# Two-layer graph network: the second feed-forward's residual and bias accumulated by TensorE beside its second product

## The chip, the cores and the metric

One core of a Trainium2 chip runs the whole program in one launch. The metric is the device time in microseconds, from start to end of the launch; lower is better. TensorE multiplies matrices (its weight loads are listed apart, as PEld), VectorE (DVE), ScalarE (ACT) and GpSimd (POOL) do the elementwise work, and SyncE (SP) issues most DMAs. Results of TensorE land in PSUM, eight banks of 512 f32 per partition.

## What is computed

3125 nodes with 128 features and 53125 edges go through two attention layers over the graph, each followed by a feed-forward block and a layer norm. The change sits in the second layer's last part:

```
h   = _ln(conv + x, g1, b1)                       # first norm
ffn = gelu(h @ Wf1 + bf1) @ Wf2 + bf2             # 128 -> 512 -> 128
y   = _ln(ffn + h, g2, b2)                        # second norm
out = _layernorm(x + y)                           # output norm
```

_ln subtracts the mean over the 128 features, divides by the root of the variance plus 1e-5, multiplies by g and adds b. x is the second layer's input. Everything is f32.

## The kernel before

Nodes are padded to 25 tiles of 128 (NB = 25), one node tile per block of 128 columns in X, Y and AGG; the text calls such a tile a node. "Quads" are groups of four nodes (the seventh has one). Every engine has its own instruction list, written out by hand; the order between engines is set by semaphores. `after(engine, name, n)` makes an engine wait until the semaphore has reached n, and an engine runs its list in order, so whatever stands behind a wait waits too.

For each of the two layers the program projects, gathers edges (26 rounds, the bulk of the time), sums them per node into AGG, and then runs the feed-forward over the nodes as a software pipeline: each engine has a loop over s, and handles node s plus or minus an offset in it. In the second layer the pieces are these.

- TensorE (loop `for s in range(-2, NB + 7)`): `widen(s+1)` (L956) makes the 512 hidden values of a node, four matmuls of 128x128 into one of two banks; `turn2(s+2)` (L951) transposes a normalised node into PS[1]; `attention` (L884) transposes the sums of a quad into PS[0], at every fourth s; `narrow(s)` (L964) is the second product, four matmuls accumulated into PS[6] (`ffn_of`). narrow waits for the gelus of its node and for `ffn_added` of the node before, since there is one tile for all.
- ScalarE: `turned2(s+1)` (L731) copies the transposed node with gain and bias of the first norm into hT2, `gelus(s)` (L739) makes four gelus, `normal2(s+5)` (L751) normalises a node in Y, with a shift that VectorE made, and `normalise_last(s-11)` (L758) makes the output rows.
- GpSimd: `inverse_root(i, b, w)` (L488) turns the variances of a quad into inverse roots, for norm 0, 1 and 2 (a, b and c in the semaphores' names); `affine(s+1)` (L538) multiplies Y by g1 and adds FB (b1 plus bf2, summed once at the end of layer one), which makes the residual in place, after turn2 has read the node.
- VectorE: `residual` (L1373), at every fourth s, adds the transposed sums of four nodes to the layer's input, takes their statistics (`node_stats`, L1384) and moments (`moments`, L1387); `add_ffn(s-1)` (L1412) adds the product in PSUM to Y and takes statistics; `scale_last(s-5)` (L1449) subtracts the mean and multiplies by g2; `add_input(s-6)` (L1454) multiplies by the inverse root, adds x and takes the statistics of the output norm; `shift_of` (L1397) makes minus mean times root for ScalarE.

`add_first_nodes` on VectorE belongs to the end of the edge rounds: it finishes the sums of the last round and already does the residual of the first two quads. SyncE stores output rows as ScalarE finishes them. The loop of the first layer shares turn2, widen, narrow and add_ffn by l == 0.

`skip_part` (L984) and `attention` of the first layer add a bias through TensorE: `ones3`, three rows, by the bias split into three bf16 parts, broadcast to 512 columns, ahead of f32 matmuls into the same bank.

Of the kernel before, what the change touches and what calls it, by code (L numbers as in the profile page):

```python
# [16 lines left out]
P = 128  # L17
# [26 lines left out]
def build(nc, a, out):  # L44
# [11 lines left out]
    with ExitStack() as ctx:  # L56
# [3 lines left out]
        def sem(name):  # L60
# [121 lines left out]
        attention_of, turned2_of, ffn_of, turned_of = PS[0], PS[1][:, 0:P], PS[6][:, 0:P], PS[7][:, 0:P]  # L182
# [13 lines left out]
            pc_ready act_col count_turned ga_ready last_oh_ready last_copy last_col fb_made x_pair skip_ready skip_added  # L196
# [253 lines left out]
        def _(pool):  # L450
# [36 lines left out]
            for l in range(2):  # L487
# [50 lines left out]
                def affine(n):  # L538
                    at = slice(n * P, (n + 1) * P)
                    after(pool, "tp2_ready", NB + n + 1)  # L540
                    g.tensor_tensor(Y[:, at], Y[:, at], GB[:, 0, :], ALU.mult).then_inc(S["ln_affine"], 1)
                    after(pool, "ln_affine", 2 * n + 1)
                    g.tensor_tensor(Y[:, at], Y[:, at], FB[:, 1, :], ALU.add).then_inc(S["ln_affine"], 1)

                inverse_root(0, *quads[0])
                inverse_root(0, *quads[1])
                if l == 0:
                    for s in range(-3, NB + 8):
# [8 lines left out]
                    pool.wait_ge(S["weights_loaded"], 16 * WEIGHTS)  # L557
# [15 lines left out]
        def _(act):  # L573
# [18 lines left out]
            for l in range(2):  # L592
# [153 lines left out]
                def normal2(n):  # L746
                    at, one = slice(n * P, (n + 1) * P), slice(n, n + 1)
                    if n % 4 == 0:
                        b, w = quads[n // 4]
                        after(act, "shift_a", b + w)  # L750
                    sc.activation(Y[:, at], Y[:, at], ACT.Identity, bias=SHIFT[0][:, one], scale=ROOT[0][:, one]).then_inc(S["xn2_ready"], 1)  # L751

# [17 lines left out]
                else:  # L770
                    for s in range(-5, NB + 11):
# [4 lines left out]
                        if in_nodes(s + 5):  # L776
                            normal2(s + 5)
# [5 lines left out]
        def _(pe):  # L783
# [12 lines left out]
            for l in range(2):  # L796
# [215 lines left out]
        def _(dve):  # L1012
# [76 lines left out]
            for l in range(2):  # L1089
# [260 lines left out]
                def add_first_nodes():  # L1350
# [3 lines left out]
                    for q in range(4):  # L1354
# [8 lines left out]
                        elif q == 1:  # L1363
                            if l:
                                shift_of(0, *quads[0])
                            else:
# [3 lines left out]
                        elif l and q == 3:  # L1370
                            shift_of(0, *quads[1])
# [15 lines left out]
                def moments(i, b, w):  # L1387
# [5 lines left out]
                    if i == 1:  # L1393
                        aggregated[b // 4] = aggregates.n
# [17 lines left out]
                def add_ffn(n):  # L1412
                    at = slice(n * P, (n + 1) * P)
                    after(dve, "ffn_ready", NB * l + n + 1)
                    if l == 0:
                        after(dve, "x_summed", n + 1)
                        v.tensor_tensor(X[:, at], ffn_of, X[:, at], ALU.add).then_inc(S["ffn_added"], 1)
                    else:
                        after(dve, "ln_affine", 2 * n + 2)
                        v.tensor_tensor(Y[:, at], ffn_of, Y[:, at], ALU.add).then_inc(S["ffn_added"], 1)  # L1420
                    after(dve, "ffn_added", NB * l + n + 1)
                    node_stats(Y if l else X, n)
                    if quad_ended(n):
                        moments(1, *quads[n // 4])

# [23 lines left out]
                def scale_last(n):  # L1449
                    at = slice(n * P, (n + 1) * P)  # L1450
                    after(dve, "aggr_step", aggregated[n // 4])
                    v.scalar_tensor_tensor(Y[:, at], Y[:, at], MOM[1][:, n, 0:1], GB[:, 2, :], ALU.subtract, ALU.mult).then_inc(S["ln_last"], 1)  # L1452

                def add_input(n):  # L1454
# [5 lines left out]
                    v.scalar_tensor_tensor(X[:, at], Y[:, at], ROOT[1][:, n:n + 1], X[:, at], ALU.mult, ALU.add).then_inc(S["x_out"], 1)  # L1460
                    after(dve, "x_out", n + 1)
# [34 lines left out]
                for s in range(-3, NB + 13):  # L1496
                    if in_nodes(s - 1):
                        add_ffn(s - 1)
                    if l == 0:
                        if s + 3 > 1 and in_nodes(s + 3):  # L1500
# [73 lines left out]
```

## Time and profile before

| | |
|---|---|
| median of 3 runs | 1337.78 us (1332.6 to 1339.69) |
| profiled execution | 1336.3 us |
| its span in the trace | 1334.5 us |
| granted clock of TensorE, mean | 0.79 |
| busy: TensorE / weight loads | 878.6 us (66%) / 769.3 us (58%) |
| busy: VectorE | 1031.2 us (77%) |
| busy: ScalarE | 747.2 us (56%) |
| busy: GpSimd | 997.2 us (75%) |
| instructions | 24923 |

The span runs from the first to the last instruction of the trace; 1.8 us of the profiled execution lie around it. Busy time is time in which an engine executes; the records of TensorE overlap by their pipelining, so starts are the better measure there. A granted clock of 1.00 is 2.4 GHz and 0.50 is 1.2 GHz. Of an f32 matmul of 128x128 the trace has two records, of a transpose one: a row with x8 is four matmuls. Each row names a line of the code, an engine, an operation and the tiles (KV also holds hT2 and the gelus in this stage, which borrow its space). Idle time with an arrow names what ended it.

### The profile page before, as it was taken

What the parts mean: (1) busy time and instruction counts of PE and PEld (TensorE: products, weight loads), DVE (VectorE), ACT (ScalarE), POOL (GpSimd) and SP (SyncE); (2) the same over time, 40 slices, a digit from 0 to 9 for tenths busy, and PEclk for the clock granted to TensorE, in tenths of its full rate; (3) what the DMA queues carried; (4) which work ended last, traced back from release to release, by engine and by line L of the source; (5) the groups of instructions that cost most, each with busy time, mean ns of one, the idle gap of its engine ahead of it and who ended that gap; (6) DMA issues with size and microseconds to landing.
All of it is one profiled execution on the core that took longest, in us unless ns stands there. A gap on an engine that the chain in (4) does not pass through costs nothing. (4 is left out here: it accounts for less than half of the span.)

```text
span 1334.5 us, 24923 instructions
## 1 busy us (share of the span) xinstructions
PE 878.6 (66%) x5107; PEld 769.3 (58%) x5107; DVE 1031.2 (77%) x2702; ACT 747.2 (56%) x2536; POOL 997.2 (75%) x1840
## 2 busy tenths in 40 slices
PE   5536546556556565568995676677686687677784
PEld 2336545545455455467874566566576576566674
DVE  5747877868768678796765888988988888889676
ACT  4315666575565664665540465655655655656775
POOL 5688888888888888833348888888888888884254
PEclk9767777687676676779998787887887888878798
DMA  7679777777777777750137788788888888885001
GB/s 208 196 203 298 242 235 242 229 224 248 223 235 243 218 244 227 221 174 1 56 122 233 246 261 278 254 251 281 247 267 277 247 264 280 268 247 165 1 1 49
DMA packets 227725, 280.51 MB, mean 210 GB/s; under 512 B 48261, under 2 KB 176419, under 8 KB 224118
## 3 DMA queue, kind: packets, MB, share of 16 engines
q1 hardware_dynamic: 185808, 167.97, 40.6%
q0 software_dynamic: 39936, 109.11, 27.3%
q10 hardware_dynamic: 1830, 1.86, 0.5%
q8 instruction: 42, 0.69, 0.2%
q14 instruction: 109, 0.89, 0.2%
HBM read 239.72 MB, written 39.08 MB: 209 GB/s over the span
## 5 line engine op out<-in xcount | busy, mean ns | idle before, releaser
L521 POOL DMA_INDIRECT KV<-kv_table,idx x832 | 800.2, 962 | 166.9 <-issue 153.8
L835 PE MATMUL PS<-QW,OHT 128*128 128x128 f32 x1664 | 299.9, 338 | 162.8 <-DVE PR L1135 143.0
L835 PEld LDWEIGHTS PS<-QW,OHT 128*128 128x128 f32 x1664 | 268.4, 243 | 183.6 <-issue 177.8
L661 ACT ACTIVATE AGG<-AGG,PC,RCS x800 | 309.3, 387 | 2.3 <-ACT AGG L657 1.5
L880 PE MATMUL PS<-OH,KV 128*128 128x128 f32 x1600 | 241.9, 308 | 30.3 <-ACT AGG L661 28.0
L880 PEld LDWEIGHTS PS<-OH,KV 128*128 128x128 f32 x1600 | 225.9, 222 | 44.8 <-issue 41.5
L1135 DVE TENSOR_TENSOR PR<-KV,PS 128x512 f32<-128x512 f32 x208 | 140.4, 675 | 119.0 <-DMA KV<-kv_table,idx 117.2
L657 ACT ACTIVATE AGG<-PS 128x127 f32 x800 | 207.9, 260 | 1.0 <-issue 0.9
L1128 DVE TENSOR_TENSOR KV<-KV,PS 128x1024 f32<-128x1024 f32 x104 | 125.5, 1206 | 65.9 <-DMA KV<-kv_table,idx 50.8
L653 ACT ACTIVATE PC<-PS 128x4 f32<-128x4 f32 x200 | 33.6, 168 | 238.4 <-PE PS L880 211.7
L855 PE MATMUL PS<-ident,AL 128*128 128x128 f32 x52 | 24.1, 464 | 199.5 <-DVE AL L1222 199.4
L491 POOL TENSOR_TENSOR ROOT<-VAR,minus_half 128x4 f32<-128x4 f32 (+1 forms) x42 | 40.0, 954 | 141.0 <-DVE VAR L1395 141.0
L1142 DVE TENSOR_REDUCE Ls<-PR 128x32 f32<-128x512 f32 x208 | 139.6, 671 | 0.3
L845 PE MATMUL PS<-We,EA 128*128 128x256 f32 x416 | 134.9, 471 | 0.0
L855 PEld LDWEIGHTS PS<-ident,AL 128*128 128x128 f32 x52 | 9.3, 179 | 212.3 <-DVE AL L1222 212.3
L1247 DVE TENSOR_TENSOR KV<-KV,PS 128x512 f32<-128x512 f32 x208 | 128.6, 679 | 0.2 <-PE PS L855 0.2
L845 PEld LDWEIGHTS PS<-We,EA 128*128 128x128 f32 x416 | 97.0, 251 | 14.7
L523 POOL MEMSET pause<- 128x1 f32 x832 | 105.0, 126 | 0.2
L683 ACT ACTIVATE RCS<-PS 128x16 f32<-128x16 f32 x52 | 9.5, 182 | 161.7 <-PE PS L859 161.7
L638 ACT ACTIVATE OHT<-REL,minus_part 128x1024 f32<-128x1024 bf16 x52 | 59.0, 1134 | 21.7 <-PE PS L835 21.7
L969 PE MATMUL PS<-W,KV 128*128 128x128 f32 x400 | 56.2, 286 | 10.4 <-ACT KV L739 6.1
L969 PEld LDWEIGHTS PS<-W,KV 128*128 128x128 f32 x400 | 52.1, 199 | 18.5 <-ACT KV L739 10.9
(162 smaller groups left out, 1331.0 us busy)
## 6 DMA issues: line engine op xcount, KB each, us to landing
QW<-q_table SPq DMA_DIRECT2D x832, 64.0 KB
REL<-rel_dram SPq DMA_DIRECT2D x52, 512.0 KB, 5.2
window_dram<-OH SPq DMA_DIRECT2D x25, 1024.0 KB
OH<-window_dram SPq DMA_DIRECT2D x50, 512.0 KB, 7.2
KV<-kv_table,idx POOLq DMA_INDIRECT x832
EA<-in_edge_batch SPq DMA_DIRECT2D x52, 256.0 KB
kv_table<-KV SPq DMA_DIRECT2D x24, 256.0 KB, 2.2
q_table<-KV SPq DMA_DIRECT2D x24, 128.0 KB, 2.2
```

What stands on the lines that cost most here:

```text
L521: g.indirect_dma_start(KV[:, s, j, :], None, kv_table, bass.IndirectOffsetOnAxis(ap=idx[:, s, j:j + 1], axis=0)).then_inc(gathered[s][hh], 16)
L523: g.memset(pause[:, l * T + n * J + j:l * T + n * J + j + 1], 0.0)
L657: sc.activation(AGG[:, ds(at + 1, P - 1)], bank[:, m, 1:P], ACT.Copy).then_inc(S["act_col"], 1)
L661: sc.activation(AGG[:, ds(at, 1)], AGG[:, ds(at, 1)], ACT.Identity, bias=PC[:, m:m + 1], scale=RCS[:, n % SLOTS, j:j + 1]).then_inc(S["act ...
L835: last = te.matmul(o, OHT[:, q // 2, e0:e0 + P], QW[:, n % 2, 4 * q + m, :], start=True, stop=True)
L845: last = te.matmul(PS[2 + q % 2][:, 2 * m * D:2 * (m + 1) * D], EA[:, e0:e0 + P], We[:, :], start=True, stop=True)
L880: last = te.matmul(PS[4 + q % 2][:, m * P:(m + 1) * P], KV[:, n % SLOTS, j, D:2 * D], at[:, j * P:(j + 1) * P], start=True, stop=True)
L969: last = te.matmul(ffn_of, gT[k][:, c, :], W2[l][:, c, :], start=(c == 0), stop=(c == 3))
L1128: v.tensor_tensor(kv, kv, ep, ALU.add).then_inc(S["e_used"], 1)
L1135: v.tensor_tensor(PR[:, q % 2, :].rearrange("p (j d) -> p j d", j=4), KV[:, n % SLOTS, 4 * q:4 * q + 4, 0:D], PS[q % 2][:, :].rearrange("p ...
L1142: v.tensor_reduce(Ls[:, :].rearrange("p (h j) -> p j h", h=H)[:, 4 * q:4 * q + 4, :], PR[:, q % 2, :].rearrange("p (j h c) -> p j h c", j= ...
L1247: v.tensor_tensor(v4, v4, at, ALU.mult).then_inc(S["pv_ready"], 1)
```

## The change

The residual and the bias of the second layer's feed-forward no longer go over GpSimd and VectorE. Ahead of each widen, TensorE starts the product's accumulation with two matmuls (`skipped`): a row of ones by FB (the bias bf2), and the turned, scaled node hT2 by the identity, which is h with its gain and bias. narrow then adds its four products. The tile rotates over four banks (PS[6], PS[7], PS[4], PS[5]), and TensorE waits for `scale_last` of the node four back in place of `ffn_added`. VectorE takes the statistics from PSUM (`ffn_stats`, `ffn_moments`) and scale_last reads PSUM, four iterations earlier than before; add_input is one iteration earlier and its statistics are a function of their own. ScalarE's normal2 goes to GpSimd, as one `tensor_scalar` per node (subtract, multiply); affine and the sum of FB and GB are gone, and so are the shifts of norm 0.

```
@@ GpSimd
-                def affine(n):
+                def normal2(n):
                     at = slice(n * P, (n + 1) * P)
-                    after(pool, "tp2_ready", NB + n + 1)
-                    g.tensor_tensor(Y[:, at], Y[:, at], GB[:, 0, :], ALU.mult).then_inc(S["ln_affine"], 1)
-                    after(pool, "ln_affine", 2 * n + 1)
-                    g.tensor_tensor(Y[:, at], Y[:, at], FB[:, 1, :], ALU.add).then_inc(S["ln_affine"], 1)
+                    if n % 4 == 0:
+                        b, w = quads[n // 4]
+                        after(pool, "root_a", NB * l + b + w)
+                    g.tensor_scalar(Y[:, at], Y[:, at], MOM[0][:, n, 0:1], ROOT[0][:, n:n + 1], ALU.subtract, ALU.mult).then_inc(S["xn2_ready"], 1)
 
                 inverse_root(0, *quads[0])
-                inverse_root(0, *quads[1])
                 if l == 0:
+                    inverse_root(0, *quads[1])
...
-                    g.tensor_tensor(FB[:, 1, :], FB[:, 1, :], GB[:, 1, :], ALU.add).then_inc(S["fb_made"], 1)
                 else:
-                    after(pool, "fb_made", 1)
+                    normal2(0)
+                    inverse_root(0, *quads[1])
                     for s in range(-4, NB + 9):
                         if quad_ended(s - 1):
                             inverse_root(1, *quads[(s - 1) // 4])
-                        if quad_ended(s - 6):
-                            inverse_root(2, *quads[(s - 6) // 4])
-                        if in_nodes(s + 1):
-                            affine(s + 1)
+                        if quad_ended(s - 5):
+                            inverse_root(2, *quads[(s - 5) // 4])
+                        if in_nodes(s + 5):
+                            normal2(s + 5)
@@ ScalarE
-                def normal2(n):
-                    at, one = slice(n * P, (n + 1) * P), slice(n, n + 1)
-                    if n % 4 == 0:
-                        b, w = quads[n // 4]
-                        after(act, "shift_a", b + w)
-                    sc.activation(Y[:, at], Y[:, at], ACT.Identity, bias=SHIFT[0][:, one], scale=ROOT[0][:, one]).then_inc(S["xn2_ready"], 1)
...
-                        if in_nodes(s + 5):
-                            normal2(s + 5)
@@ TensorE
+                def skipped(n, k):
+
+                    o = ffn_of[1][n % 4]
+                    if n == 0:
+                        pe.wait_ge(S["fb_loaded"], 16)
+                        after(pe, "rcs_ready", 2 * G)
+                    if n == 1:
+                        after(pe, "pv_ready", 8 * G)
+                    if n == 2:
+                        after(pe, "last_copy", 2 * J)
+                    after(pe, "ln_last", n - 3)
+                    te.matmul(o, ones[:, :], FB[0:1, 1, :], start=True, stop=False)
+                    te.matmul(o, hT2[k], ident[:, :], start=False, stop=False)
+
                 def widen(n):
                     k = n % 2
                     after(pe, "ht2_ready", NB * l + n + 1)
+                    if l:
+                        skipped(n, k)
...
-                    after(pe, "ffn_added", NB * l + n)
+                    if l == 0:
+                        after(pe, "ffn_added", n)
                     for c in range(4):
-                        last = te.matmul(ffn_of, gT[k][:, c, :], W2[l][:, c, :], start=(c == 0), stop=(c == 3))
+                        last = te.matmul(ffn_of[l][n % 4], gT[k][:, c, :], W2[l][:, c, :], start=(l == 0 and c == 0), stop=(c == 3))
@@ VectorE
+                def ffn_stats(n):
+                    after(dve, "ffn_ready", NB + n + 1)
+                    stats.step(v.bn_stats(BN[:, n, :], ffn_of[1][n % 4]))
+
+                def ffn_moments(n):
+
+                    after(dve, "stat_step", stats.n)
+                    aggregates.step(v.bn_aggr(MOM[1][:, n, :], BN[:, n, :]))
+                    aggregated[n] = aggregates.n
...
-                    v.scalar_tensor_tensor(Y[:, at], Y[:, at], MOM[1][:, n, 0:1], GB[:, 2, :], ALU.subtract, ALU.mult).then_inc(S["ln_last"], 1)
+                    v.scalar_tensor_tensor(Y[:, at], ffn_of[1][n % 4], MOM[1][:, n, 0:1], GB[:, 2, :], ALU.subtract, ALU.mult).then_inc(S["ln_last"], 1)
+                    if quad_ended(n):
+                        b, w = quads[n // 4]
+                        v.tensor_scalar(VAR[1][:, b:b + w], MOM[1][:, b:b + w, 1], EPS, None, ALU.add).then_inc(S["var_b"], w)
...
                     else:
-                        if quad_at(s + 7) and s > 0:
-                            shift_of(0, *quad_at(s + 7))
+                        if in_nodes(s - 1):
+                            ffn_stats(s - 1)
+                        if quad_at(s - 9):
+                            shift_of(2, *quad_at(s - 9))
+                        if in_nodes(s - 1):
+                            ffn_moments(s - 1)
                         if in_nodes(s - 5):
-                            scale_last(s - 5)
-                        if in_nodes(s - 6):
-                            add_input(s - 6)
-                        if quad_at(s - 10):
-                            shift_of(2, *quad_at(s - 10))
+                            add_input(s - 5)
+                        if in_nodes(s - 1):
+                            scale_last(s - 1)
+                        if in_nodes(s - 5):
+                            input_stats(s - 5)
                     if quad_at(s + 8) and s >= 0:
                         residual(*quad_at(s + 8))
```

`input_stats` is the second half of the former add_input: statistics of X and, at the end of a quad, their moments.

## Rows read from the trace of the kernel before

**Rows 1.** Windows from 1250: length, busy us (x count) of engines, clock, DMA

```profile
1250.00:1260.00 10.00, 8.43 (x38) 8.03 (x39) 5.06 (x23) 4.97 (x16) 4.72 (x8) 0.50 0.01 2
1260.00:1280.50 20.50, 17.61 (x155) 17.19 (x155) 12.92 (x57) 16.81 (x54) 10.39 (x18) 1.00 0.00 1
1280.50:1284.00 3.50, 3.50 (x18) 3.21 (x17) 3.05 (x15) 1.28 (x5) 1.56 (x3) 0.51 0.01 5
1284.00:1317.60 33.60, 28.48 (x236) 26.52 (x235) 27.50 (x123) 28.70 (x90) 20.46 (x38) 1.00 0.06 17
1317.60:1334.50 16.90, 0.02 (x1) 0.00 (x0) 7.95 (x39) 3.68 (x9) 4.05 (x5) 0.62 0.22 64
```

**Rows 2.** Timeline of PE, 1249 to 1320: start, length, line, operation

```profile
1256.80 1.91 PE L969 MATMUL PS<-W,KV 128*128 128x128 f32 x8
...
1262.17 1.06 PE L969 MATMUL PS<-W,KV 128*128 128x128 f32 x8
1263.07 1.06 PE L961 MATMUL PS<-KV,W 128*128 128x128 f32 x8
1263.96 0.27 PE L954 MATMUL PS<-ident,Y 128*128 128x128 f32 x1
1264.07 0.60 PE L903 MATMUL PS<-ident,AGG 128*128 128x128 f32 x4
1264.51 1.06 PE L969 MATMUL PS<-W,KV 128*128 128x128 f32 x8
...
1279.61 1.14 PE L969 MATMUL PS<-W,KV 128*128 128x128 f32 x8 [1.85 <-DVE Y L1420]
...
1316.49 1.13 PE L969 MATMUL PS<-W,KV 128*128 128x128 f32 x8 [0.55 <-DVE Y L1420]
```

**Rows 3.** Waits, 1257 to 1317.6: total us, times, longest

```profile
PE PS L969 <- DVE Y L1420: 4.1, 6, 1.9
PE PS L969 <- ACT KV L739: 3.7, 3, 1.9
```

**Rows 4.** Timeline, 1276 to 1290, DVE

```profile
1276.97 0.67 DVE L1378 TENSOR_TENSOR Y<-PS,Y 128x512 f32<-128x512 f32 x1
...
1279.17 0.29 DVE L1420 TENSOR_TENSOR Y<-PS,Y 128x128 f32<-128x128 f32 x1
```

**Rows 5.** Lines from 1250: count, busy us, mean ns, idle before

```profile
L491 POOL TENSOR_TENSOR ROOT<-VAR,minus_half 128x4 f32<-128x4 f32 x17 | 17.2, 1013 | 31.8 <-DVE VAR L1395 31.8
L751 ACT ACTIVATE Y<-Y,SHIFT,ROOT 128x128 f32<-128x128 f32 x23 | 11.7, 512 | 3.0 <-DVE SHIFT L1400 3.0
L541 POOL TENSOR_TENSOR Y<-Y,GB 128x128 f32<-128x128 f32 x25 | 11.6, 466 | 4.0 <-PE PS L954 4.0
...
L543 POOL TENSOR_TENSOR Y<-Y,FB 128x128 f32<-128x128 f32 x25 | 11.4, 457 | 2.0
L1385 DVE BATCH_NORM_STATS2 BN<-Y 128x6 f32<-128x128 f32 x42 | 11.1, 289 | 1.0
...
L1420 DVE TENSOR_TENSOR Y<-PS,Y 128x128 f32<-128x128 f32 x25 | 7.2, 287 | 11.1 <-PE PS L969 9.2 <-POOL Y L543 1.9
...
L491 POOL TENSOR_TENSOR ROOT<-VAR,minus_half 128x1 f32<-128x1 f32 x3 | 1.7, 568 | 0.7 <-DVE VAR L1395 0.7
```

**Rows 6.** Timeline of PE, 693.5 to 700.8, first and second layer between

```profile
695.72 0.39 PE L990 MATMUL PS<-BIAS,ones 3*128 3x512 bf16 x1
696.04 1.16 PE L993 MATMUL PS<-Wp,AGG 128*128 128x128 f32 x8
697.13 0.38 PE L990 MATMUL PS<-BIAS,ones 3*128 3x512 bf16 x1
```

**Rows 7.** Timeline, 1244 to 1334.5: ACT and POOL at both edges

```profile
1248.87 1.64 ACT L751 ACTIVATE Y<-Y,SHIFT,ROOT 128x128 f32<-128x128 f32 x4
...
1250.20 1.01 POOL L491 TENSOR_TENSOR ROOT<-VAR,minus_half 128x4 f32<-128x4 f32 x1 [2.77 <-DVE VAR L1395]
...
1326.78 2.03 ACT L758 ACTIVATE Y<-X,SHIFT,ROOT 128x128 f32<-128x128 f32 x5 [3.01 <-DVE SHIFT L1400]
```

More of the change, by code:

```diff
@@ L181, in build @@
         logits_t, alpha_t = PS[6][:, 0:P], PS[7][:, 0:P]
-        attention_of, turned2_of, ffn_of, turned_of = PS[0], PS[1][:, 0:P], PS[6][:, 0:P], PS[7][:, 0:P]
+        attention_of, turned2_of, turned_of = PS[0], PS[1][:, 0:P], PS[7][:, 0:P]
+        ffn_of = [[PS[b][:, 0:P] for b in banks] for banks in ((6,) * 4, (6, 7, 4, 5))]
         S = {n: sem(n) for n in """x_loaded0 x_loaded1 x_loaded2 x_loaded3 dst_loaded dste_loaded gates_in first_weights fb_loaded weights_loaded late_weights
@@ L195, in build @@
             alpha_done rc_done rcd_done at_ready rce_ready rcs_ready oh_ready pv_ready agg_ready
-            pc_ready act_col count_turned ga_ready last_oh_ready last_copy last_col fb_made x_pair skip_ready skip_added
+            pc_ready act_col count_turned ga_ready last_oh_ready last_copy last_col  x_pair skip_ready skip_added
             xn2_ready tp2_ready ht2_ready aggr_step var_a var_b var_c root_a root_b root_c shift_a shift_c
@@ L770, in _ @@
                 else:
-                    for s in range(-5, NB + 11):
+                    for s in range(-1, NB + 11):
                         if in_nodes(s + 1):
@@ L1363, in add_first_nodes @@
                         elif q == 1:
-                            if l:
-                                shift_of(0, *quads[0])
-                            else:
+                            if l == 0:
                                 normal2(0)
@@ L1369, in add_first_nodes @@
                             residual(*quads[1])
-                        elif l and q == 3:
-                            shift_of(0, *quads[1])
                 def residual(b, w):
@@ L1392, in moments @@
                     after(dve, "aggr_step", aggregates.n)
-                    if i == 1:
-                        aggregated[b // 4] = aggregates.n
                     v.tensor_scalar(VAR[i][:, b:b + w], MOM[i][:, b:b + w, 1], EPS, None, ALU.add).then_inc(S["var_" + LNS[i]], w)
@@ L1413, in add_ffn @@
                     at = slice(n * P, (n + 1) * P)
[L1414 to L1422, printed above, removed]
+                    after(dve, "ffn_ready", n + 1)
+                    after(dve, "x_summed", n + 1)
+                    v.tensor_tensor(X[:, at], ffn_of[0][n % 4], X[:, at], ALU.add).then_inc(S["ffn_added"], 1)
+                    after(dve, "ffn_added", n + 1)
+                    node_stats(X, n)
                     if quad_ended(n):
                         moments(1, *quads[n // 4])
+                def ffn_stats(n):
[5 more added lines that the diff above has]
+                    aggregated[n] = aggregates.n
                 def next_normal(n):
@@ L1450, in scale_last @@
                     at = slice(n * P, (n + 1) * P)
-                    after(dve, "aggr_step", aggregated[n // 4])
-                    v.scalar_tensor_tensor(Y[:, at], Y[:, at], MOM[1][:, n, 0:1], GB[:, 2, :], ALU.subtract, ALU.mult).then_inc(S["ln_last"], 1)
+                    after(dve, "aggr_step", aggregated[n])
+                    v.scalar_tensor_tensor(Y[:, at], ffn_of[1][n % 4], MOM[1][:, n, 0:1], GB[:, 2, :], ALU.subtract, ALU.mult).then_inc(S["ln_last"], 1)
+                    if quad_ended(n):
+                        b, w = quads[n // 4]
+                        v.tensor_scalar(VAR[1][:, b:b + w], MOM[1][:, b:b + w, 1], EPS, None, ALU.add).then_inc(S["var_b"], w)
                 def add_input(n):
@@ L1460, in add_input, with input_stats @@
                     v.scalar_tensor_tensor(X[:, at], Y[:, at], ROOT[1][:, n:n + 1], X[:, at], ALU.mult, ALU.add).then_inc(S["x_out"], 1)
+                def input_stats(n):
                     after(dve, "x_out", n + 1)
@@ L1496, in _ @@
                 for s in range(-3, NB + 13):
-                    if in_nodes(s - 1):
-                        add_ffn(s - 1)
                     if l == 0:
+                        if in_nodes(s - 1):
+                            add_ffn(s - 1)
                         if s + 3 > 1 and in_nodes(s + 3):
```

2 lines of the change are left out of this document (1 added, 1 removed).

## The prediction

> **What bounds it now.** I began with the page: 1334.5 us of span, VectorE busiest, no engine near full. The diff touches only the second layer's feed-forward, which follows its edges, so the next view is the busy time by stretch [rows 1]: from 1250 to the end, 84.5 us, 6% of the span. All that the change can give or cost lies there. Up to 1317.6 TensorE is the fullest engine, at the lower clock (0.50) until about 1260 and again from 1280.5 to 1284, else at the full one.
>
> The timeline of TensorE [rows 2] shows how. While it runs freely, one node takes from 1262.17 to 1264.07: narrow (4 matmuls) 0.90, widen (4 more) 0.89, turn 0.11, together 1.90 us. Every fourth node adds four turns of the attention sums, 0.44 (1264.07 to 1264.51). But from narrow(0) at 1256.80 to narrow(24) at 1316.49 stand 59.7 us. Full-clock work in it is 47 groups of 0.893 (42.0; 8 records of 0.1117), 22 turns (2.4) and the attention turns (1.4), 45.8. The two stretches at half clock add half of their lengths (3.3 and 3.5 us), 3.4. The remaining 10.5 us is waiting.
>
> The waits [rows 3] say for whom: narrow waits for L1420, VectorE's addition of node n-1, since all nodes share one PSUM tile, and for the gelus, which come late behind a delayed round. The origin is visible once per four nodes [rows 4]: at 1276.97 VectorE starts the residual, statistics and moments of the next four nodes and reaches the finished product only at 1279.17, 2.2 us later; narrow stands until 1279.61 [rows 2]. Thus TensorE is the bound, with about 0.4 us per node of stalls caused by VectorE's burst.
>
> **The change, part by part.**
>
> *Removed stall.* The product rotates over four PSUM banks and narrow no longer waits for VectorE. What remains is scale_last(n-4) before skipped(n). VectorE starts scale_last about 0.8 us after the product (statistics, aggregate and add_input, an estimate from the 0.29 us rows), 1.1 with its run, plus a burst of 2.2 and moments of some 0.9 when it is behind; between the end of narrow(n-4) and skipped(n) TensorE has two full nodes, at least 3.8 us. This wait should stay hidden, with little to spare. ScalarE loses normal2 (L751, 512 ns each [rows 5], 0.4 from start to start), so its per-node load falls from about 2.2 to 1.8 and gelus are ready in time. Of the 10.5 us I leave 0.5, the last gelu group before narrow(24), which has no widen to cover it: -10.0.
>
> *Added on TensorE.* Two f32 matmuls per node of 128 columns (ones by the bias row, hT2 by ident): two quarters of 0.893, 0.445 us. Of the 25 pairs, 23 fall between narrow(0) and narrow(24): +10.2. The gain and this price cancel almost exactly.
>
> *The matmul with one input row.* The trace has no f32 matmul of one row. The nearest is the bias matmul of three rows (L990, bf16, 512 columns) ahead of 128-row ones [rows 6]. It repeats every 1.41 us (695.72 to 697.13). Columns alone give 0.223 + 0.893 = 1.12. So going to a three-row matmul and back costs 0.29, in part ahead of it and in part behind. The bounds are 0, if one row of f32 behaves like a full matmul, and 0.6, if each of the two passes that an f32 matmul is recorded as pays it. I take 0.29, from the same engine and kind of operand: 23 times 0.29, +6.7. The Trainium skill, TensorEngine Tiling (Array Packing), section Key Properties, states that changing the tiling mode drains TensorE; by that rule, the trace agrees, with 1.41 against 1.12 us. The skill's TensorE: Matmul & The Clock Gate, LDWEIGHTS, has the load go by columns and not by input rows; taken alone it would leave out the 6.7.
>
> *Clock.* Of the 3.4 us, the second dip follows the 1.85 us stall at 1279.61. Without stalls I expect none there, and at the start TensorE works without a gap from about 1252 instead of 1254.7, so the full clock may come by about 1257 instead of 1260: -3.2 (the ends are 0 and -3.4).
>
> *VectorE.* It loses the 25 additions of 287 ns and the shifts of the first norm; stats and scale_last read PSUM instead of SBUF. L1420 reads PSUM in 287 ns and the statistics from SBUF take 289 [rows 5], so I give PSUM no surcharge (ends -0.05 and +0.1 us each, covered). Its load was 43.5 us of the 57.6 between 1260 and 1317.6 [rows 1] and falls to some 36 of 62; the aggregates, now issued one node at a time, have add_input laid between them and their reader. Cost 0, covered by TensorE's 2.7 us per node.
>
> *GpSimd.* It loses L541 and L543 (466 and 457 ns) and gets one tensor_scalar per node. No such row on GpSimd exists; 466 ns for a two-input 128x128 is nearest, 1013 ns for the power of 128x4 the upper end. With three roots per four nodes (3.0 us) it has 4.9 to 7.1 of TensorE's 10.9 us. normal2 is issued five nodes ahead, so nothing is late: 0. The addition FB + GB at the end of layer one goes too, 0.5 us ahead of a wait for stores: 0.
>
> *Start.* Today ScalarE normalises four nodes (1248.87 to 1250.41 [rows 7]) before it can serve the first turned tile. Afterwards GpSimd does node 0 during ScalarE's last copies and widen(0) can start near 1250.2 instead of 1250.9. But node 1 stands behind GpSimd's second root, done at 1251.2 [rows 7], and TensorE has two skipped parts more at half clock. narrow(0) comes out at 1256.4: -0.4.
>
> *End.* From narrow(24) to ScalarE's last row (1316.49 to 1328.81 [rows 2, 7]) are 12.3 us. Afterwards nodes 20 to 23 are already scaled when it starts. Laid out from narrow(24): statistics of 24 at 1.7; the shift of nodes 16 to 19 waits for two roots of 1.0 in a row, to 3.1; add_input(20), scale_last(24), then four pairs of add_input and statistics at about 0.58 (twice a 0.29 us row, each waiting for the other) to 5.9; moments to 6.8; root to 7.9; node 24 with its moments and root (568 ns) to 9.8; shift and ScalarE to 10.5. So -1.8. The 5.7 us of output behind it stay.
>
> **Sum**, against the profiled execution of 1336.3 us (span 1334.5): -10.0 + 10.2 + 6.7 - 3.2 - 0.4 - 1.8 = +1.5. That execution lies 1.5 below the median of 1337.78; the four known times (1332.6, 1336.3, 1337.78, 1339.69) average 1336.6. Adding 1.5 to the average and half of its distance to the median gives 1338.7.
>
> **Rivals.** About 0.5%, 6.7 us, is what measurement can tell from no change.
>
> A, the forecast: TensorE becomes continuous but longer, +1.5 (chance 0.50; 1334 to 1343 for itself). B: the one-row matmul costs only its columns, -5.2, about 1332. For it: f32 passes among themselves pipeline in every group of rows 2; against it: all three-row repeats in rows 6 show the extra (0.20). C, the other side: both f32 passes pay, 0.6 per node, +8.6, about 1345.8. It decides above roughly 0.5 us per skipped part; place: ahead of each widen, 23 times. The bf16 row cannot exclude it (0.15). D: GpSimd's tensor_scalar is so slow that it bounds. It decides above (10.9 - 3.0) / 4 = 2.0 us each; at 2.5 it would add 6 times 2.0, +12, to A. Against it is every 128x128 row at under 0.6 us (0.05). E: the change doesn't do what it says, because the stall only moves to the wait on scale_last or on shifts of the output norm; a burst longer by 2 us stalls five times 1 us or so, +6.5 (0.10).
>
> **Chances.** Faster by over 0.5% needs B with a further early clock, or the mean's luck: a third of B, a little of A, 0.12. Slower: most of C, all of D, a third of E, a little of A: 0.20. Same: 0.68. The range leaves out D and the outer part of C and B: 1331 to 1346.
>
> **What would show it.** TensorE between narrow(0) and narrow(24) nearly without idle, 2.6 to 2.7 us per node, more with attention; skipped part 0.7 to 0.8 us from its first start to widen's; no dip of the clock after 1257 to 1260 until the end; no wait of PE for VectorE; GpSimd's new row near 0.5 us; last ScalarE row 10.5 us behind narrow(24). A skipped part of 0.45 makes B right, of 1.0 C; PE waiting on ln_last in the list of waits makes E right; roots and normal2 filling GpSimd make D right.

## The result, and the profile after

The kernel with the change takes 1343.76 us (median of 8 runs, 1339.38 to 1346.34) beside 1337.49 for the one before (8 runs, 1332.6 to 1340.04): a ratio of 1.0041, with an interval of [1.0027, 1.0055]. By the ratio that is 5.5 us longer, and within the 0.5% that the prediction called the same. The profiled execution took 1345.9 us, 1344.2 of them span, against 1336.3 and 1334.5 before. Of these 9.7 us of span, 4.3 lie ahead of the stage: the last group of matmuls of the edge rounds (L871, before L880) starts at 1249.87 instead of 1245.59. The edge rounds hold no edit, and single executions differ by as much: in the traces of all the runs below, that group starts between 1245.59 and 1250.54. From that group to the end it is 94.3 us instead of 88.9: +5.4, which agrees with the ratio's difference. So the effect can be read in the stage's trace.

The page's first part, of after. VectorE lost 11 us of work and TensorE gained 12, of which the sum's two matmuls are most:

```profile
PE 890.3 (66%) x5207; PEld 775.0 (58%) x5207; DVE 1020.0 (76%) x2670; ACT 737.8 (55%) x2511; POOL 997.5 (74%) x1814
```

Windows of after (length, then busy us of TensorE, its weight loads, VectorE, ScalarE, GpSimd, then granted clock, DMA share, GB/s), which answer to [rows 1]:

```profile
1254.00:1256.00 2.00, 1.29 (x10) 1.10 (x10) 1.11 (x6) 0.00 (x0) 1.82 (x3) 1.00 0.00 0
1256.00:1258.00 2.00, 1.94 (x7) 1.38 (x7) 1.31 (x5) 1.47 (x5) 2.00 (x4) 0.54 0.00 0
1258.00:1262.00 4.00, 4.00 (x19) 4.00 (x19) 1.57 (x10) 1.27 (x6) 3.21 (x5) 0.50 0.00 0
1262.00:1264.00 2.00, 2.00 (x12) 1.57 (x12) 0.83 (x3) 0.24 (x1) 1.28 (x2) 0.76 0.00 0
1264.00:1328.00 64.00, 63.66 (x495) 58.16 (x494) 35.46 (x173) 39.77 (x130) 25.37 (x29) 1.00 0.03 9
```

From 1264 to 1328 TensorE is busy for 63.66 of 64 us at the full clock, while no other engine is above 40. The stalls of before are gone; what TensorE is given to do is now the length of the stage. The price of it stands in the timeline of TensorE, which answers to [rows 2]:

```profile
1260.51 1.92 PE L977 MATMUL PS<-W,KV 128*128 128x128 f32 x8
...
1264.38 1.06 PE L977 MATMUL PS<-W,KV 128*128 128x128 f32 x8
1265.37 0.48 PE L958 MATMUL PS<-FB,ones 1*128 1x128 f32 x2
1265.78 0.49 PE L959 MATMUL PS<-ident,KV 128*128 128x128 f32 x2
1266.11 1.06 PE L968 MATMUL PS<-KV,W 128*128 128x128 f32 x8
...
1267.11 1.06 PE L977 MATMUL PS<-W,KV 128*128 128x128 f32 x8
...
1327.09 1.16 PE L977 MATMUL PS<-W,KV 128*128 128x128 f32 x8 [0.34 <-ACT KV L739]
```

Read the starts. A node takes 2.73 us (1264.38 to 1267.11), and it took 1.90 before. The columns of the two added matmuls (L958 and L959) account for 0.445 of the 0.83. The other 0.39 is spread over three places: narrow ahead of the one-row matmul now lasts 0.99 instead of 0.90, the one-row matmul (L958) lasts 0.41 where its columns are worth 0.22, and the identity matmul behind it (L959) 0.33 instead of 0.22. narrow(0) to narrow(24) is 66.58 us instead of 59.69. The timeline of the weight loads (PEld) shows what changes there:

```profile
1265.37 0.29 PEld L958 LDWEIGHTS PS<-FB,ones 1*128 1x128 f32 x2
1265.78 0.30 PEld L959 LDWEIGHTS PS<-ident,KV 128*128 128x128 f32 x2
```

The load of the one row takes as long as that of 128 rows, but both loads start together with their matmuls (1265.37 and 1265.78), and not ahead of them.

The waits of after, from 1256 to 1328 (total us, times, longest), answer to [rows 3]:

```profile
DVE BN L1426 <- PE PS L977: 29.1, 18, 2.7
...
PE PS L977 <- ACT KV L739: 0.3, 1, 0.3
```

TensorE never waits for VectorE; VectorE waits 29 us for TensorE. TensorE's only other wait is one of 0.8 us for GpSimd, at the start (L945). The lines from 1250 on (busy us, mean ns, idle before), as in [rows 5], show what the new operations cost:

```profile
L544 POOL TENSOR_SCALAR Y<-Y,MOM,ROOT 128x128 f32<-128x128 f32 x25 | 19.8, 801 | 0.1
...
L1460 DVE SCALAR_TENSOR_TENSOR Y<-PS,MOM,GB 128x128 f32<-128x128 f32 x25 | 8.6, 345 | 0.1
...
L1426 DVE BATCH_NORM_STATS2 BN<-PS 128x6 f32<-128x128 f32 x25 | 7.4, 297 | 29.4 <-PE PS L977 29.1
...
L1389 DVE BATCH_NORM_STATS2 BN<-X 128x6 f32<-128x128 f32 x25 | 7.1, 285 | 0.1
```

GpSimd's tensor_scalar takes 0.80 us, and VectorE pays almost nothing for PSUM (297 ns against 285). Last, VectorE's burst, once per four nodes, as in [rows 4]:

```profile
1284.62 0.69 DVE L1382 TENSOR_TENSOR Y<-PS,Y 128x512 f32<-128x512 f32 x1
...
1286.82 0.29 DVE L1426 BATCH_NORM_STATS2 BN<-PS 128x6 f32<-128x128 f32 x1
...
1287.51 0.34 DVE L1460 SCALAR_TENSOR_TENSOR Y<-PS,MOM,GB 128x128 f32<-128x128 f32 x1
```

The burst still delays a node, number 8, whose statistics come at 1286.82 and whose bank is free at 1287.85. The bank's next user is node 12, whose skipped part starts at 1290.79: 2.9 us to spare in the worst round.

### The profile page after: what moved, and what is told of

Same layout as the page of the kernel before. It is cut to its first block and busy times, and to the rows that moved or that the text cites. A ratio compares the mean times of both kernels' runs of the same rounds, so it can differ in the third digit from the quotient of the medians.

```text
span 1344.2 us, 24976 instructions
## 1 busy us (share of the span) xinstructions
PE 890.3 (66%) x5207; PEld 775.0 (58%) x5207; DVE 1020.0 (76%) x2670; ACT 737.8 (55%) x2511; POOL 997.5 (74%) x1814
## 3 DMA queue, kind: packets, MB, share of 16 engines
q0 software_dynamic: 39936, 109.11, 27.4%
## 5 line engine op out<-in xcount | busy, mean ns | idle before, releaser
L826 PE MATMUL PS<-QW,OHT 128*128 128x128 f32 x1664 | 306.9, 344 | 174.7 <-DVE PR L1143 153.9
L826 PEld LDWEIGHTS PS<-QW,OHT 128*128 128x128 f32 x1664 | 274.5, 249 | 198.3 <-issue 192.9
L871 PE MATMUL PS<-OH,KV 128*128 128x128 f32 x1600 | 228.7, 296 | 28.2 <-ACT AGG L661 25.4
L871 PEld LDWEIGHTS PS<-OH,KV 128*128 128x128 f32 x1600 | 212.5, 211 | 42.2 <-issue 39.2
L524 POOL MEMSET pause<- 128x1 f32 x832 | 101.8, 122 | 0.2
L1245 DVE TENSOR_TENSOR OH<-PS,rel_edge 128x1024 f32<-128x1024 f32 x50 | 60.9, 1217 | 0.0
L640 ACT ACTIVATE OHT<-OHT,one_col 128x1024 f32<-128x1024 f32 x52 | 59.7, 1148 | 1.7
```

The source lines that it names most:

```text
L524: g.memset(pause[:, l * T + n * J + j:l * T + n * J + j + 1], 0.0)
L826: last = te.matmul(o, OHT[:, q // 2, e0:e0 + P], QW[:, n % 2, 4 * q + m, :], start=True, stop=True)
L871: last = te.matmul(PS[4 + q % 2][:, m * P:(m + 1) * P], KV[:, n % SLOTS, j, D:2 * D], at[:, j * P:(j + 1) * P], start=True, stop=True)
L1245: v.tensor_tensor((last_windows if n == G - 1 else OH)[:, hh * 8 * P:(hh + 1) * 8 * P].rearrange("p (m n) -> p m n", m=8), iota_psum[:, :] ...
```

## The experiments

My theory after this reading: with four banks the stage is bound by TensorE alone, so each microsecond taken from or given to its node shows in full; and 0.39 us per node is the price of going to a one-row matmul and back. Rivals are named with each run. Times are medians; a ratio is to the kernel before on the same chip. In every diff the lines are those of the kernel after, unless said otherwise.

**The bias by a matmul of full height (full_rows).** The bias is in every row of FB, so the identity as the weight gives the same sum.

```
-                    te.matmul(o, ones[:, :], FB[0:1, 1, :], start=True, stop=False)
+                    te.matmul(o, ident[:, :], FB[:, 1, :], start=True, stop=False)
```

> Only edit to the changed kernel: the bias matmul has 128 rows (identity by the broadcast bias) in place of one row. Theory (the one-row matmul makes TensorE change its mode and pay 0.39 us per node beyond its columns; in the trace of the changed kernel L958 takes 0.41 and narrow and L959 0.10 more each): the node falls from 2.73 to 2.34 us, 25 nodes give -9.7, so about 1334 against 1343.8, and 3 us below the kernel before. Rival (two more matmuls cost what they cost, whatever their rows; the rest of the loss is GpSimd's 0.80 us normalisation and VectorE reading PSUM): the same as the changed kernel, 1343 to 1345.

Measured: 1329.93 us (1328.77 to 1336.81), ratio 0.9949 [0.9932, 0.9965]. That is 0.92% or 12.3 us below the kernel with the change, and 0.5% faster than the one before. Timeline of TensorE:

```profile
1309.02 1.06 PE L977 MATMUL PS<-W,KV 128*128 128x128 f32 x8
1309.91 0.39 PE L958 MATMUL PS<-FB,ident 128*128 128x128 f32 x2
1310.13 0.39 PE L959 MATMUL PS<-ident,KV 128*128 128x128 f32 x2
1310.36 1.06 PE L968 MATMUL PS<-KV,W 128*128 128x128 f32 x8
```

and of its weight loads:

```profile
1309.80 0.30 PEld L958 LDWEIGHTS PS<-FB,ident 128*128 128x128 f32 x2
1310.03 0.30 PEld L959 LDWEIGHTS PS<-ident,KV 128*128 128x128 f32 x2
```

Narrow lasts 0.89 again and both skipped matmuls 0.22 each: the node is 2.34 us, 0.39 less. Each load now starts 0.10 to 0.11 ahead of its matmul, under the matmul before it. narrow(0) to narrow(24) is 56.6 us, 10.0 below the 66.6: 23 times 0.39 is 9.0, and the full clock from the first narrow on gives the rest. Narrow(0) also stands 9.2 us behind the last group of the edge rounds instead of 10.6.

**No bias matmul at all (no_bias).** It leaves the bias bf2 out of the result.

```
-                    te.matmul(o, ones[:, :], FB[0:1, 1, :], start=True, stop=False)
-                    te.matmul(o, hT2[k], ident[:, :], start=False, stop=False)
+                    te.matmul(o, hT2[k], ident[:, :], start=True, stop=False)
```

> The changed kernel without the bias matmul at all; it leaves out the second layer's bf2. Theory: beside the mode change of 0.39 the columns of one f32 matmul go, 0.223 us, so the node takes 2.12 us and the time is 25 times 0.61 = 15 below the changed kernel, about 1328.5, and 5.6 below the one with 128 rows. VectorE and GpSimd are then still below TensorE's time. Rival (another engine bounds soon below 2.7 us per node): the gain stops early, 1334 or more.

Measured: 1327.13 us (1322.95 to 1329.31), ratio 0.9917 [0.9897, 0.9937]. By the ratios it is 4.3 us below full_rows, where 5.6 were expected; by the trace narrow(0) to narrow(24) is 51.45 us, 5.15 less, which is 23 times the 0.22 of the columns. Timeline of TensorE, a node of 2.12 us:

```profile
1304.96 1.06 PE L976 MATMUL PS<-W,KV 128*128 128x128 f32 x8
1305.86 0.39 PE L958 MATMUL PS<-ident,KV 128*128 128x128 f32 x2
...
1307.08 1.06 PE L976 MATMUL PS<-W,KV 128*128 128x128 f32 x8
```

So the theory holds in both: the one-row form costs 0.39 beyond its columns, and TensorE's columns are still the bound below it.

**Where the price arises (half_rows, one_row_twice, before_widen).** Three kernels of which each ran once, on one chip whose kernel before has a median of 1339.63; they are there for their traces. The last two add bf2 twice.

```
# half_rows
+        part64 = sb("part64", [64, P])       # filled with 1/64
-                    te.matmul(o, ones[:, :], FB[0:1, 1, :], start=True, stop=False)
+                    te.matmul(o, part64[:, :], FB[0:64, 1, :], start=True, stop=False)
# one_row_twice: between the two matmuls of skipped; before_widen: behind both
+                    te.matmul(o, ones[:, :], FB[0:1, 1, :], start=False, stop=False)
```

> The changed kernel with a bias matmul of 64 rows: 64 rows of 1/64 by 64 rows of the broadcast bias. Theory (TensorE pays for leaving the full-height form of matmul, not for the count of rows as such): the same extra as with one row, node 2.73 us, the bias part 0.41 to its successor. Rival (only a short operand of few rows pays): 2.34 us per node as with 128 rows.

> The changed kernel with its one-row matmul issued twice in a row, so it adds bf2 twice. Theory (the price is for going there and back): the second costs its columns alone, 0.22 us, and the node takes 2.95 us. Rival (each one-row matmul, or each of its two records, pays for itself): 0.41 or more on top, 3.14 us per node.

> The same second one-row matmul, but behind the identity matmul and ahead of widen, so that TensorE goes there and back twice per node; it adds bf2 twice. Theory: 0.22 for the columns and 0.39 for the second way there and back, node 2.73 + 0.61 = 3.34 us. Rival (no price of place): 2.95 us, as with the two side by side.

Measured: half_rows 1343.49 us, one_row_twice 1347.19, before_widen 1358.92. The timelines of TensorE, in this order:

```profile
1291.46 0.48 PE L960 MATMUL PS<-FB,part 64*128 64x128 f32 x2
1291.88 0.49 PE L961 MATMUL PS<-ident,KV 128*128 128x128 f32 x2
...
1294.19 0.49 PE L960 MATMUL PS<-FB,part 64*128 64x128 f32 x2
```

```profile
1292.54 0.48 PE L958 MATMUL PS<-FB,ones 1*128 1x128 f32 x2
1292.87 0.38 PE L959 MATMUL PS<-FB,ones 1*128 1x128 f32 x2
1293.18 0.49 PE L960 MATMUL PS<-ident,KV 128*128 128x128 f32 x2
...
1295.49 0.48 PE L958 MATMUL PS<-FB,ones 1*128 1x128 f32 x2
```

```profile
1292.54 0.48 PE L958 MATMUL PS<-FB,ones 1*128 1x128 f32 x2
1292.96 0.49 PE L959 MATMUL PS<-ident,KV 128*128 128x128 f32 x2
1293.37 0.48 PE L960 MATMUL PS<-FB,ones 1*128 1x128 f32 x2
...
1295.88 0.48 PE L958 MATMUL PS<-FB,ones 1*128 1x128 f32 x2
```

Sixty-four rows cost what one costs: a node of 2.73 us, 0.42 for the bias part. A second one-row matmul right behind the first adds only its columns (2.95 against 2.73, +0.22). The same matmul put behind the identity one, so that TensorE goes and comes back twice, adds 0.61 (3.34). So the price belongs to the way there and back, 0.39 per trip, the same for 1 row and for 64, and the same for one matmul and for two in the trip. With the weight loads above, the likely reading is that a load doesn't overlap with the matmul before it when the height changes; why TensorE does so, no run shows.

**The rotation alone, without TensorE's sum (rotate_only).** The kernel before, with four banks and narrow waiting for the addition of the node four back; all else as before.

```
-                    after(pe, "ffn_added", NB * l + n)
+                    if l == 0:
+                        after(pe, "ffn_added", n)
+                    else:
...
+                        after(pe, "ffn_added", NB + n - 3)
                     for c in range(4):
-                        last = te.matmul(ffn_of, gT[k][:, c, :], W2[l][:, c, :], start=(c == 0), stop=(c == 3))
+                        last = te.matmul(ffn_of[l][n % 4], gT[k][:, c, :], W2[l][:, c, :], start=(c == 0), stop=(c == 3))
```

> The kernel before with one part of the change: its second product rotates over four PSUM banks and narrow waits for the addition of the node four back instead of the last one. Nothing is added to TensorE. Theory (of the 10.5 us of waiting in the old loop most comes from the one shared tile): 6 to 9 us below the kernel before, 1329 to 1331. Rival (VectorE with addition, scaling and the burst, at 43.5 us busy of 57.6, is the bound behind the tile, and GpSimd's two passes too): only 0 to 3 us below, 1335 to 1337.

Measured: 1336.62 us (1331.23 to 1338.56), ratio 0.9989 [0.9976, 1.0002]. The theory's 6 to 9 us did not come; the rival was right. narrow(0) to narrow(24) is 56.96 us, only 2.7 less than before, and the end is 1.2 longer. The timelines of TensorE, of ScalarE and of GpSimd show the wait that took the old one's place:

```profile
1286.77 2.00 PE L962 MATMUL PS<-KV,W 128*128 128x128 f32 x8 [2.24 <-ACT KV L732]
```

```profile
1285.88 0.49 ACT L759 ACTIVATE Y<-X,SHIFT,ROOT 128x128 f32<-128x128 f32 x1 [2.64 <-DVE SHIFT L1410]
1286.28 0.44 ACT L732 ACTIVATE KV<-PS,gb 128x128 f32<-128x128 f32 x1
```

```profile
1284.40 1.01 POOL L492 TENSOR_TENSOR ROOT<-VAR,minus_half 128x4 f32<-128x4 f32 x1 [1.96 <-DVE VAR L1405]
```

Widen waits for the copy of the turned node (L732), which stands on ScalarE behind an output row (L759) that waits 2.64 us for VectorE's shift. That shift needs GpSimd's root, which VectorE's late variance lets start only at 1284.40 and which takes 1.01 us of the 2.64. From 1256 to 1312 TensorE waits 5.4 us for L732 in 4 waits, and ScalarE 5.0 for the shift. VectorE, with its additions, is busy for 38.05 of the 52 us from 1260 to 1312, and for 33.60 in full_rows, where TensorE is busy for 52.00 of 52. So behind the stall on the single tile stood a second one, in a chain through VectorE's burst, GpSimd's root and ScalarE's row. The change takes both away. Which of its other parts does it isn't shown: the additions leave VectorE, the two passes of `affine` leave GpSimd (VectorE's additions waited 1.9 us for them [rows 5]), and VectorE's scaling and output norm come earlier. The place of the first norm isn't the reason: with it back on ScalarE (normal_on_act, below) the steady part is as short.

**Fewer banks (three_banks, two_banks).** How much of the rotation is needed:

```
-        ... for banks in ((6,) * 4, (6, 7, 4, 5))]
+        ... for banks in ((6,) * 3, (6, 7, 4))]      # two_banks: (6,) * 2, (6, 7)
-                    after(pe, "ln_last", n - 3)
+                    after(pe, "ln_last", n - 2)      # two_banks: n - 1
```

with n % 3 (n % 2) in place of n % 4.

> The changed kernel with three PSUM banks in the rotation. In its trace scale_last of the node behind a burst ends at 1287.85 and a three-bank skipped part would start at 1288.06. Theory (four banks are one more than this loop needs): no difference from the changed kernel, 1342 to 1345. Rival (the wait on scale_last is tight): 0.5 us or more per quad, 3 us and up.

> The changed kernel with two banks. skipped(n) then stands directly behind narrow(n-2) and needs VectorE's scale_last of that node. Theory: 1.2 us of TensorE's time per plain node and 2.5 behind a burst, 3 times 1.2 + 2.5 = 6 us per quad, some 30 to 36 us above the changed kernel, 1374 to 1380. Rival (rotation isn't what removed the waits): near 1344.

Measured: three_banks 1342.81 us (1340.06 to 1345.34), ratio 1.0036 [1.002, 1.0051], the same as four; two_banks 1370.88 (1369.75 to 1373.13), ratio 1.0249 [1.0221, 1.0277], 27.8 us above the kernel with the change by the ratios (30 to 36 expected). The waits of two_banks from 1256 on:

```profile
PE PS L958 <- DVE Y L1460: 27.4, 23, 1.4
```

With two banks TensorE waits in 23 nodes for the scaling, 27.4 us, which is all of the difference. With three it doesn't wait for it once.

**The start (start_order).** full_rows with GpSimd's normal2(1) ahead of its second root, on POOL:

```
                     normal2(0)
+                    normal2(1)
                     inverse_root(0, *quads[1])
...
-                        if in_nodes(s + 5):
+                        if s > -4 and in_nodes(s + 5):
```

> The kernel with the 128-row bias, and GpSimd normalises node 1 before it takes the second quad's root instead of after it. In the changed kernel turn2(1) waits for GpSimd until 1256.06, 0.8 us after widen(0), and ScalarE stands 3.1 us. Theory (that wait sets the start of the loop): 0.8 to 1.5 us below the run with the 128-row bias alone. Rival (TensorE is held at the start by half clock and the attention of the third quad anyway): no difference.

Measured: 1331.09 us (1328.68 to 1332.39), ratio 0.995 [0.9932, 0.9968]; no difference from full_rows (0.9949). Timeline of TensorE:

```profile
1250.27 0.80 PE L959 MATMUL PS<-FB,ident 128*128 128x128 f32 x2 [0.69 <-ACT KV L732]
...
1251.28 1.91 PE L969 MATMUL PS<-KV,W 128*128 128x128 f32 x8
```

The edit did take away the wait for node 1, 0.96 us in full_rows. But in this execution the granted clock was 0.55 to 0.60 from 1250 to 1254, behind idle times of 1.71 and 0.69 us, so the first widen took 1.91 us and narrow(0) stands 9.1 us behind the last group of the edge rounds, as before (9.2). In bf16_rows below, with the same order, idle times of 1.79 and 0.69 us and the full clock, it is 7.3. So the order may give up to some 1.7 us where the clock stays up (an estimate: 9.2 less 7.3, less 0.2 for the shorter bias parts of two nodes); the medians, with some 2 us to either side, can't tell.

**Is GpSimd the better place for the first norm? (normal_on_act, normal_on_act_again).** full_rows with normal2 back on ScalarE and the shifts of norm 0 back on VectorE; the second run is the same kernel once more.

```
-                    normal2(0)      # POOL
...
-                        if in_nodes(s + 5):      # POOL
-                            normal2(s + 5)
...
+                        if in_nodes(s + 5):      # ACT, as in the kernel before
+                            normal2(s + 5)
...
+                        if quad_at(s + 7) and s > 0:      # DVE
+                            shift_of(0, *quad_at(s + 7))
```

> The kernel with the 128-row bias, and one part of the change undone: the first norm goes back from GpSimd to ScalarE, with the shifts on VectorE. Theory (TensorE bounds at 2.34 us per node; ScalarE would stand at 2.1, VectorE gets 0.1 back): the same as the run with the 128-row bias within 2 us, perhaps 1 us worse where four normalisations stand ahead of the first turned tile. Rival (moving the norm to GpSimd carries part of the gain): 3 to 6 us slower than that run.

> The kernel of normal_on_act once more, on what may be another chip. In its first comparison it stood 0.36% above full_rows by the two ratios to the kernel before (0.9985 against 0.9949), though its own trace has the stage from narrow(0) to narrow(24) as long as full_rows' (56.58 against 56.6 us) and only narrow(0) later, by 1.5 us. Theory 1, that the stage's trace tells the whole of it and the rest was scatter between comparisons: ratio 0.995 to 0.997, that is 4 to 6.5 us below the kernel before. Theory 2, that moving the first norm to ScalarE costs 4 to 5 us somewhere that the one profile doesn't show: ratio 0.998 to 1.000 again.

Measured: 1335.07 us (1330.79 to 1339.89), ratio 0.9985 [0.997, 1.0], and 1335.47 (1331.51 to 1337.45), ratio 0.9979 [0.9966, 0.9992]. So by the ratios it is worse than full_rows by 4.0 to 4.8 us, twice, and my theory that the traces tell the whole of it with 1.5 us fell. The steady part is as long (56.58 and 56.59 us against 56.6), and ScalarE has room for it. The cost is at the start, and the second trace shows more of it than the first. The timeline of TensorE of normal_on_act_again:

```profile
1252.05 0.33 PE L951 MATMUL PS<-ident,Y 128*128 128x128 f32 x1 [2.69 <-ACT Y L748]
1253.54 0.80 PE L964 MATMUL PS<-FB,ident 128*128 128x128 f32 x2 [1.17 <-ACT KV L728]
...
1254.56 1.91 PE L974 MATMUL PS<-KV,W 128*128 128x128 f32 x8
```

The same in full_rows:

```profile
1250.06 0.33 PE L945 MATMUL PS<-ident,Y 128*128 128x128 f32 x1 [2.09 <-POOL Y L544]
1251.07 0.49 PE L958 MATMUL PS<-FB,ident 128*128 128x128 f32 x2 [0.69 <-ACT KV L731]
...
1251.62 1.06 PE L968 MATMUL PS<-KV,W 128*128 128x128 f32 x8
```

ScalarE normalises four nodes before it serves the first turned tile, as it did in the kernel before [rows 7]: 3.9 us of idle TensorE ahead of the first widen instead of 2.8, and that widen, at half clock, takes 1.91 us by its row instead of 1.06. The half clock needn't come from the edit, since start_order's trace has it too. From the last group of the edge rounds to narrow(0) it is 10.7 and 11.5 us in the two traces and 9.2 in full_rows. From that group to the end of the span, full_rows has 82.8 us and these have 84.7 and 85.6: 1.9 to 2.8 of the 4.0 to 4.8 are seen. Each ratio has an interval of some 0.15%, 2 us, to either side, so the rest may be no more than that; it stays open.

**The bias in bf16 (bf16_rows).** full_rows with start_order's edit; GpSimd, while it waits in the edge rounds' end, splits the bias into three bf16 parts that add up to it and lays them in the first three rows of a tile BZ of 128 rows, the others zero.

```
-                    te.matmul(o, ident[:, :], FB[:, 1, :], start=True, stop=False)
+                    te.matmul(o, ones128[:, :], BZ[:, :], start=True, stop=False)      # both bf16
```

> The kernel with the 128-row bias and node 1 ahead of the root, with the bias split once by GpSimd, in its long wait, into three bf16 rows of a 128-row bf16 tile whose other rows are zero; a 128-row tile of bf16 ones multiplies it. Theory (TensorE still bounds; a bf16 pass of 128 columns takes 0.056 us against 0.223): 0.17 us less per node, 25 of them 4.2 us, so 1326 to 1327. The run without the bias matmul stood at 1327.1, so no further than that. Rival (near 2.2 us per node VectorE's bursts come back): no difference from 1330 to 1331.

Measured: 1331.18 us (1327.09 to 1332.1) where the kernel before had 1339.63, ratio 0.9929 [0.991, 0.9947]. It is the best complete version, though its interval overlaps that of full_rows; by the ratios it is 2.7 us below it, where 4.2 were expected. Timeline of TensorE:

```profile
1291.21 0.22 PE L975 MATMUL PS<-BZ,ones 128*128 128x128 bf16 x1
1291.26 0.44 PE L976 MATMUL PS<-ident,KV 128*128 128x128 f32 x2
1291.54 1.06 PE L985 MATMUL PS<-KV,W 128*128 128x128 f32 x8
```

The skipped part is 0.33 us instead of 0.45 and the node 2.22, so a node gives 0.12 and not the 0.17 of the theory: narrow(0) to narrow(24) is 53.95 us, 2.6 less. The change of type between full-height matmuls costs 0.06 behind it (0.28 for L976), little beside the 0.39 of the one-row form.

## Why the prediction was right, step by step

It named 1338.7 us, 1331 to 1346, and no difference as likeliest; the median is 1343.76, inside the range but 0.8 above the 1334 to 1343 that rival A, the forecast, had for itself. The mechanism was the one forecast (TensorE continuous but longer, the gain paid back by its own added work). The sum said +1.5 and the trace +5.4.

- **Removed stall, -10.0.** Right as a sum: 0.34 us in the steady part is left, 0.5 was given. But the reason named, the shared tile, was the smaller part of it. Rotate_only took the tile's wait away and won 2.7 us between the two narrows; the rest came with the other parts of the change, the relief of VectorE and GpSimd and the new order, which the prediction had booked at nothing and which no run takes apart. That this term came out is in part luck: the change holds them all.
- **Two matmuls by their columns, +10.2.** Right: 0.22 us each in full_rows, and no_bias gives 5.15 back for one of the two.
- **One-row mode change, +6.7.** This is the term that failed, by its size: 0.39 us per node and not 0.29, so +9.0. The 0.29 came from a bf16 row with three rows and 512 columns [rows 6]; for f32 there is 0.10 ahead, 0.19 on it and 0.10 behind. The row was the nearest and its bounds of 0 and 0.6 held the value. The skipped part came out at 0.74 us, in the 0.7 to 0.8 that was to show it; the missing 0.10 lay ahead of it, in narrow, where the sign I had named doesn't look. The Trainium skill, TensorEngine Tiling (Array Packing), Key Properties, has TensorE drain at a change of tiling mode. If a matmul of fewer than 128 rows counts as such a change, half_rows and one_row_twice agree, with 0.39 us for 64 rows as for one, and only 0.22 for a second matmul in the same mode. The Trainium skill, TensorE: Matmul & The Clock Gate, LDWEIGHTS, has the load's time go by columns and not by rows; the trace agrees, with 0.29 us for the two loads of one row and 0.30 for those of 128. What that leaves out is when the load starts, and there the 0.39 us arise.
- **Clock, -3.2.** The second dip did go. At the start the clock fell at about 1256, behind waits of 1.56, 0.69 and 0.77 us, and was full again only at about 1263, not at 1257 to 1260; the gain was about 2.1 (2.5 us at half clock behind narrow(0) cost 1.25 of the 3.4). In full_rows it didn't fall there at all, behind waits as long, so this term scatters from run to run, and its size in one trace is partly chance.
- **VectorE, 0.** Right: 35.46 us busy of 64 ("some 36 of 62"), PSUM no dearer. The margin of the wait on scale_last was called small; three_banks shows that it is more than one whole node.
- **GpSimd, 0.** The cost of an instruction was wrong, 0.80 us and not 0.466, but inside its bounds; GpSimd is busy for 25.4 of the 64 us, so the cover held.
- **Start, -0.4** came out as -0.6 (11.2 to 10.6 us from the last group of matmuls of the edge rounds to narrow(0)). **End, -1.8**: ScalarE's last row ends 10.3 us behind narrow(24), 10.5 forecast. But the 5.7 us of output behind it did not stay: they became 6.8. That is no scatter, for all twelve traces of kernels with the change in them have 6.75 to 6.84 us there, and those of the kernel before and of rotate_only 5.69 and 5.74. The last transfer ends some 2.5 us before the end of the span in the kernel before and some 4 us in the one with the change, and no row of an engine stands in that time, so the cause stays open.

Together: +2.3 for the mode change, +1.1 for the clock, +1.1 for the output, which the sum had at nothing, -0.2 for the start, -0.2 for the end and -0.2 for what is left of the others make +3.9, the distance from +1.5 to +5.4. The sum was too low by more than its own size, and the range held because it was 15 us wide.

Of the rivals, B (only columns) fell with 0.39. C's time, 1345.8, was nearer to the measured one than the forecast's 1338.7, but its price wasn't (0.39 is nearer to 0.29 than to 0.6), and its mechanism, that each pass pays, is excluded by one_row_twice. D fell with 0.80 us against the 2.0 from which it decides. E, the stall moved to scale_last, is what two_banks does, by 27 us; with four banks its wait is never last.

## What to carry to other kernels

A gain from removed stalls ends where the engine that was stalled becomes full: whatever the same change lays on that engine is then paid at its whole price, so put it there in its cheapest form. A matmul with less than full height, between matmuls of full height, pays for the way there and back each time (0.39 us here); if the operand exists in all rows, one edit (the identity by FB) turned this change from 0.4% slower to 0.5% faster. And look for the second wait behind the first before a buffer is doubled: four banks alone gave nothing that can be told from zero.

## What of the hardware was new to me

- A trip to f32 matmuls of 1 or 64 rows and back costs 0.39 us at the full clock, of which 0.10 shows in the matmuls ahead of it. The weight loads on the trip take no longer, but start with their matmul and not 0.11 us ahead of it. A switch from f32 to bf16 and back at full height costs about 0.06.
- GpSimd's tensor_scalar with two scalars per partition takes 0.80 us for 128x128 f32, although it reads one tile, and its tensor_tensor, which reads two, takes 0.46 [rows 5]. On ScalarE the same normalisation takes 0.51.
- The granted clock fell to half in some of these starts and stayed full in others with the same idle times in front of it: 0.55 and 0.60 from 1250 to 1254 in start_order, behind 1.71 and 0.69 us, and 1.00 from 1250 to 1262 in bf16_rows, behind 1.79 and 0.69 us.
